# A graph-network kernel: splits put between ScalarE's normalising steps, half a batch norm on GpSimd, and the projection in two unrolled parts

## The reference, cut to what matters

```
h = relu(layernorm(x));  x = x + sage(relu-batchnorm of sage(h))      # two mean aggregations
h = relu(layernorm(x));  x = x + two hops of a relational layer (h)
h = relu(layernorm(x));  x = x + batchnorm(relu((h + A h) @ W1 + b1) @ W2 + b2)
h = relu(layernorm(x));  x = x + attention(h):
    w = softmax(h @ attn_w.T + attn_b);  xp = h + w @ node_anchor
    b = softmax(leaky(concat(h[src], h[dst]) @ edge_w.T + edge_b));  ep = b @ edge_anchor
    xp + 0.5 * (sum of ep at src + sum of ep at dst)
```

## Time and profile before

| | |
|---|---|
| median of 3 runs | 5902.55 us (5898.19 to 5908.68) |
| the profiled execution | 5876.22 us |
| its span in the profile | 5874.40 us |
| busy: PE, PEld, DVE, ACT, POOL | 59%, 40%, 40%, 23%, 38% |
| chain that ended last: PE, issue, POOL, DVE, ACT | 21%, 18%, 16%, 5%, 2% |

### The profile page before, as it was taken

One profiled execution on the slowest core, in us unless ns is written; L12 is line 12 of the kernel. 1 busy time (PEld: TensorE's weight loads), 2 busy tenths in 40 slices (PEclk: granted clock), 3 DMA queues, 4 the chain that ended last, 5 costly groups with the idle time before them and its releaser, 6 DMA issues.

```text
span 5874.4 us, 68831 instructions
## 1 busy us (share of the span) xinstructions
PE 3488.4 (59%) x18857; PEld 2341.4 (40%) x18858; DVE 2356.2 (40%) x6119; ACT 1354.9 (23%) x2986; POOL 2236.6 (38%) x2337
## 2 busy tenths in 40 slices
PE   5599997998633333333333333337994566655566
PEld 3255553444332222222333233333443455544455
DVE  7756566113322222222122222223116555555556
ACT  2555451001200000000000000001002555555555
POOL 3000000000366666665666666660001444444442
PEclk8699998998756666666555555558995777777777
DMA  2111113222522222222111111113220221212122
GB/s 70 52 68 46 67 45 129 94 87 87 160 56 67 69 67 67 70 66 68 46 45 46 46 46 46 46 45 115 108 87 17 44 45 43 45 41 41 43 50 53
DMA packets 264711, 371.64 MB, mean 63 GB/s; under 512 B 63252, under 2 KB 200251, under 8 KB 256299
## 3 DMA queue, kind: packets, MB, share of 16 engines
q1 hardware_dynamic: 186790, 251.51, 12.9%
q0 software_dynamic: 74464, 114.31, 8.7%
q10 hardware_dynamic: 3364, 4.69, 0.3%
HBM read 261.10 MB, written 109.21 MB: 63 GB/s over the span
## 4 chain that ended last, share of the span: by engine, by line
PE 21%; issue 18%; POOL 16%; another core or an unknown queue 9%; DVE 5%; DMA 2%; DVEq 2%; ACT 2%; ACTq 0%; POOLq 0%; SPq 0%
POOL GS L716 16%; PE psum L1296 7%; PE psum L1437 5%; PE psum L1242 3%; DMA GS<-xw_table,stage 2%; PE psum L1464 2%; DVEq L1779 1%; DVE GS L1779 1%; PE psum L1389 1%; PE psum L1390 1%; PE psum L1431 1%; PE psum L1221 1%; DVEq L1786 0%; ACT O L1056 0%
## 5 line engine op out<-in xcount | busy, mean ns | idle before, releaser
L716 POOL DMA_INDIRECT GS<-xw_table,stage x1664 | 1576.7, 948 | 2277.3 <-issue 1925.9
L1296 PE MATMUL psum<-HA,HT 128*128 128x512 fp8e4 (+1 forms) x5733 | 1253.7, 369 | 63.8 <-DVE HT L1962 63.8
L1242 PE MATMUL psum<-GS 128*128 128x96 f32 x3328 | 691.1, 382 | 712.7 <-DMA GS<-xw_table,stage 611.1
L716 POOL DMA_INDIRECT HA<-p_table,stage x624 | 603.3, 967 | 1213.6 <-DMA p_table<-HT 536.6
L1242 PEld LDWEIGHTS psum<-GS 128*128 128x128 f32 x3328 | 634.5, 287 | 765.7 <-issue 762.2
L1296 PEld LDWEIGHTS psum<-HA,HT 128*128 128x128 bf16 x5733 | 554.5, 100 | 642.8 <-DVE HT L1962 64.8
L1779 DVE TENSOR_SCALAR GS<-iota,HT,wt 128x96 f32<-128x96 f32 x1680 | 473.7, 349 | 449.8 <-issue 448.2
L1793 DVE TENSOR_TENSOR HA<-HA,psum 128x96 f32 x208 | 52.8, 254 | 1358.7 <-remote 859.4
L1221 PE MATMUL psum<-Wcat,HT 128*128 128x512 f32 x196 | 177.6, 1060 | 476.7 <-DVE HT L2255 443.4
L991 ACT ACTIVATE HA<-psum 128x392 fp8e4<-128x392 f32 x784 | 349.5, 494 | 345.5 <-PE psum L1201 332.3
L1201 PE MATMUL psum<-edge_cols 128*128 128x196 bf16 x1568 | 341.0, 351 | 39.1 <-ACT HA L991 23.6
(11 more groups left out here) (363 smaller groups left out, 4179.0 us busy)
## 6 DMA issues: line engine op xcount, KB each, us to landing
HT<-dst_rows SPq DMA_DIRECT2D x212, 256.0 KB
xw_table<-HT SPq DMA_DIRECT2D x100, 512.0 KB, 3.2
HA<-adj SPq DMA_DIRECT2D x26, 1600.0 KB, 6.3
adj<-HA SPq DMA_DIRECT2D x13, 3136.0 KB, 9.5
HA<-adj SPq DMA_DIRECT2D x26, 1536.0 KB, 9.7
GS<-xw_table,stage POOLq DMA_INDIRECT x1664
HA<-p_table,stage POOLq DMA_INDIRECT x624
h_table<-HA SPq DMA_DIRECT2D x4, 960.0 KB, 5.7
```

What stands on the lines that cost most here:

```text
L716: nc.gpsimd.indirect_dma_start(out=to, out_offset=None, in_=table, in_offset=bass.IndirectOffsetOnAxis(ap=idx, axis=0)).then_inc(done, 16)
L1242: last = nc.tensor.matmul(bank[h][:, 0:WINDOW], G3[g][:, j, :], S_pair[h][:, t, :], start=(t == 0), stop=(t == 2 * GT - 1))
L1296: last = nc.tensor.matmul(bank[s][:, 0:w], Hs4[:, b, t, :], adj_tile[s][:, b * GW:b * GW + w], start=(b == 0 and t == 0), stop=(b == SRCS ...
```

## The change

First group, splits and batch norms. `normalise_and_split` replaces `normalise` and `split` in the first and third layer: ACT normalises five blocks, splits ten, and so on, each split waiting only for the blocks that it reads. DVE no longer waits for all of `H` ahead of its part. `split(TO_SAGE2, ...)` starts when the first 25 blocks are there. POOL applies the first batch norm to blocks 25 to 49 and the second to blocks 32 to 49, while DVE does the others; the result goes straight into `H`. `O` is cleared by DVE, behind the split.

Second group, the projection. The last norm goes in two parts, blocks 0 to 27 (12 of them normalised by DVE) and 28 to 49 (12 by DVE), written out without loops. The projection takes four blocks at a time, in 13 steps, reads `H` without staging, and ACT copies the products too. `X = X + H` is one DVE step of 50 blocks.

```diff
+        blocks_in = lambda i: {PROJ: 4}.get(i, 1)
+        NORM_PARTS = ((slice(0, 28), slice(0, 12)), (slice(28, NB), slice(28, 40)))
+        BY_POOL = slice(32, NB)
...
@@ POOL
             gather_rest(REST_SAGE1, (h_table, P))
+            pool.wait_ge(bn_scaled, 1)
+            nc.gpsimd.tensor_tensor(H3[:, late_half, :], O3[:, late_half, :], in_late_half(sd[:, :]), ALU.mult).then_inc(bn_scaled, 1)
+            pool.wait_ge(bn_scaled, 2)
+            nc.gpsimd.tensor_tensor(H3[:, late_half, :], H3[:, late_half, :], in_late_half(mu[:, :]), ALU.add).then_inc(h_ready, 1)
...
-            pool.wait_ge(combined, 2 * HOP_BLOCKS)
-            nc.gpsimd.memset(O[:, :], 0.0).then_inc(rest_cleared, 1)
             gather_rest(REST_GIN, (h_table, P))
+            pool.wait_ge(bn_scaled, 3)
+            nc.gpsimd.tensor_tensor(T3[:, BY_POOL, :], T3[:, BY_POOL, :], in_blocks(sd[:, :]), ALU.mult).then_inc(bn_scaled, 1)
+            pool.wait_ge(bn_scaled, 4)
+            nc.gpsimd.tensor_tensor(X3[:, BY_POOL, :], X3[:, BY_POOL, :], T3[:, BY_POOL, :], ALU.add).then_inc(bn_scaled, 1)
@@ ACT, the projection
+            def copy_turned(m):
+                act.wait_ge(transposed, proj_before + m + 3)
+                act.wait_ge(multiplied, proj_before + m + 1)
+                nc.scalar.activation(tT[m % 2][:, 0:w], bank[6 + m % 2][:, 0:w], ACT.Copy).then_inc(t_copied, 1)
+            def copy_projected(m):
+                act.wait_ge(multiplied, proj_before + m + 3)
+                nc.scalar.activation(T[:, 4096 + m * 60:4096 + m * 60 + w], bank[2 + m % 2][:, 0:w], ACT.Copy).then_inc(evac_d, 1)
+            root_of(0)
+            normalise_four(3)
+            normalise_four(4)
+            copy_turned(0)
+            normalise_four(5)
+            copy_turned(1)
+            act.wait_ge(bn_scaled, 5)
+            copy_projected(0)
+            normalise_four(6)
+            for m in range(2, 6):
+                copy_turned(m)
+                copy_projected(m - 1)
+            root_of(1)
+            for m in range(6, 9):
+                normalise_four(m + 4)
+                copy_turned(m)
+                copy_projected(m - 1)
...
@@ PE, the projection
+            turn_normed(0)
+            for m in range(1, steps_of(PROJ)):
+                turn_normed(m)
+                project(m - 1)
+            project(steps_of(PROJ) - 1)
@@ DVE
-            wait_for_normed(1)
             split_h(TO_SAGE1)
...
-            for at, ready in zip(halves, (h_first, h_ready)):
-                ch(V.tensor_tensor(T3[:, at, :], O3[:, at, :], over_half(sd[:, :]), ALU.mult))
-                V.tensor_tensor(H3[:, at, :], T3[:, at, :], over_half(mu[:, :]), ALU.add).then_inc(ready, 1)
-            dve.wait_ge(h_ready, 2)
+            ch(V.tensor_tensor(H3[:, halves[0], :], O3[:, halves[0], :], over_half(sd[:, :]), ALU.mult))
+            V.tensor_tensor(H3[:, halves[0], :], H3[:, halves[0], :], over_half(mu[:, :]), ALU.add).then_inc(h_first, 1)
             split_h(TO_SAGE2)
...
-            wait_for_normed(4)
             split_h(TO_GIN)
-            dve.wait_ge(rest_cleared, 1)
+            dve.wait_ge(combined, 2 * HOP_BLOCKS)
+            ch(V.memset(O[:, :], 0.0))
...
-            for at in halves:
-                ch(V.tensor_tensor(T3[:, at, :], T3[:, at, :], over_half(sd[:, :]), ALU.mult))
-            ch(V.tensor_tensor(X3, X3, T3, ALU.add))
-            layer_norm()
+            dve.sem_inc(bn_scaled, 1)
+            mine = slice(0, BY_POOL.start)
+            ch(V.tensor_tensor(T3[:, mine, :], T3[:, mine, :], sd[:, :].unsqueeze(1).broadcast_to([P, mine.stop, P]), ALU.mult))
+            ch(V.tensor_tensor(X3[:, mine, :], X3[:, mine, :], T3[:, mine, :], ALU.add))
+            V.tensor_copy(iota49, iota[:, 0:49])
+            normalise_part(*NORM_PARTS[0])
+            dve.wait_ge(bn_scaled, 5)
+            normalise_part(*NORM_PARTS[1])
...
+            dve.wait_ge(h_ready, 6)
+            dve.wait_ge(h_act, 4 * NORM_ACT_STEPS + 3)
+            V.tensor_tensor(X3, X3, H3, ALU.add)
-            block_loop(PROJ, project_out, lambda b, s: V.tensor_copy(in_st[s][:, 0:2 * P], H[:, bass.ds(b * 2 * P, 2 * P)]))
+            dve.wait_ge(evac_d, steps_before(PROJ) + steps_of(PROJ) + 2)
```

More of the change, by code:

```diff
@@ L382, in gnn_stack @@
         hop_added = sem("hop_added")
-        rest_cleared = sem("rest_cleared")
+        bn_scaled = sem("bn_scaled")
         dst_in = [sem(f"dst_in{i}") for i in range(2)]
@@ L883, in stage_h @@
                 return nc.scalar.activation(in_st[s][:, 0:P], H[:, bass.ds(b * P, P)], ACT.Copy)
[L886 to L898, removed]
+            ten = lambda c: slice(c * 10, min(SRCS, c * 10 + 10))
@@ new lines, in high, with middle, normalise_and_split, five @@
+            def high(c):
+                nc.scalar.activation(Hs4[:, ten(c), 0, :], H3[:, ten(c), :], ACT.Copy).then_inc(split_high, 1)
+            def middle(q, c):
+                act.wait_ge(split_rest, 5 * q + c + 1)
+                nc.scalar.activation(Hs4[:, ten(c), 1, :], halves_of[c % 2][:, 0:ten(c).stop - ten(c).start, :], ACT.Copy).then_inc(split_mid, 1)
+            def normalise_and_split(q, norm, first, ready):
+                def five(i):
+                    for b in range(NORM_DVE + 5 * i, NORM_DVE + 5 * i + 5):
+                        last = nc.scalar.activation(H[:, b * P:(b + 1) * P], X[:, b * P:(b + 1) * P], ACT.Relu,
+                                                    bias=neg_mean[:, b:b + 1], scale=stat2[:, b:b + 1])
+                    last.then_inc(h_act, 1)
+                act.wait_ge(scales_ready, norm)
+                five(0)
+                act.wait_ge(h_first, first)
+                high(0)
+                act.wait_ge(h_ready, ready)
+                high(1)
+                middle(q, 0)
+                high(2)
+                middle(q, 1)
+                five(1)
+                act.wait_ge(h_act, NORM_ACT_STEPS * (norm - 1) + 2)
+                high(3)
+                middle(q, 2)
+                five(2)
+                five(3)
+                act.wait_ge(h_act, NORM_ACT_STEPS * norm)
+                high(4)
+                middle(q, 3)
+                middle(q, 4)
@@ L900, in turn_own, with split @@
+            def split(q, first, ready):
+                act.wait_ge(h_first, first)
+                high(0)
+                high(1)
+                middle(q, 0)
+                act.wait_ge(h_ready, ready)
+                for c in range(2, 5):
+                    high(c)
+                    middle(q, c - 1)
+                middle(q, 4)
             def turn_own(q, roots):
@@ L1034, in _ @@
             sqrt(stat2[:, :], stat[:, :], 2 * DENSE + 4)
[L1035 to L1039, removed]
+            normalise_and_split(TO_GIN, 3, 4, 4)
             relu_hidden()
@@ L1073, in _, with root_of, normalise_four @@
                 rows_ahead(0, 0, g)
-            sqrt(stat2[:, :], stat[:, :], 2 * DENSE + 6)
-            normalise(4)
+            proj_before = steps_before(PROJ)
+            def root_of(part):
+                at = NORM_PARTS[part][0]
+                sqrt(stat2[:, at], stat[:, at], 2 * DENSE + 6 + part)
+                act.wait_ge(scales_ready, 4 + part)
+            def normalise_four(m):
+                for b in projected(m):
+                    last = nc.scalar.activation(H[:, b * P:(b + 1) * P], X[:, b * P:(b + 1) * P], ACT.Relu,
+                                                bias=neg_mean[:, b:b + 1], scale=stat2[:, b:b + 1])
+                last.then_inc(h_act, 1)
+            def copy_turned(m):
+                w = len(projected(m)) * P
+                act.wait_ge(transposed, proj_before + m + 3)
+                act.wait_ge(multiplied, proj_before + m + 1)
+                nc.scalar.activation(tT[m % 2][:, 0:w], bank[6 + m % 2][:, 0:w], ACT.Copy).then_inc(t_copied, 1)
+            def copy_projected(m):
+                w = len(projected(m)) * 15
+                act.wait_ge(multiplied, proj_before + m + 3)
[17 more added lines that the diff above has]
+                copy_projected(m - 1)
+            for m in range(9, steps_of(PROJ)):
+                copy_turned(m)
+                copy_projected(m - 1)
+            copy_projected(steps_of(PROJ) - 1)
             act.wait_ge(zeros_done, 1)
```

72 lines of the change are left out of this document (50 added, 22 removed).

## The result

| | us |
|---|---|
| before, median of 20 runs | 5911.69 (5887.11 to 5918.23) |
| changed kernel, median of 20 runs | 5890.89 (5874.97 to 5904.19) |
| ratio | 0.9972, 95% interval 0.9963 to 0.9980 |
| profiled execution of the changed kernel | 5891.48 (span 5889.7) |

The ratio on record is not the quotient of the two medians, which would be 0.9965 (-20.8 us); the text goes by the recorded ratio, since it has the interval. Of 5902.55 us it is -16.5 us, with an interval of -21.8 to -11.8: faster. The forecast of 5881 (-21.6) lies at the interval's edge, and the cases of 5863.5, 5897 and 5958 lie outside.

The account below looks back on a forecast made before the run. Chains of waits, stage by stage, were taken as the bound, no engine being busy over 59%. Terms -0.6 - 8.6 + 5.3 - 17.7 = -21.6 us took the median from 5902.55 to 5881 us, range 5856 to 5892.

Parts of the forecast that it names:

- D: Second batch norm, last norm and projection: -17.7 us, with the projection starting earlier and TensorE the bound from there.
- A: Norm and split before the first layer: -0.6 us, only the earlier end of the split counting.
- B: First batch norm, shared by DVE and GpSimd: +5.3 us, since the two take turns.
- Rival 1: Both batch norms: DVE and GpSimd overlap, total -39.0 us, giving 5863.5 us; chance 0.30.
- C: Norm and split before the third layer: -8.6 us, from moving O's clearing to DVE (-3.2) and an earlier first split (-5.4).
- Taking turns from 4446.8: Second batch norm: DVE 4.4, GpSimd 4.9, DVE 4.4 us, ending at 4460.6, GpSimd's sum then beside one-input statistics.
- 50 blocks at 0.585: Projection: TensorE is the bound from its start, 0.585 us a block, 29.3 us in all.
- Rival 2: Projection becomes a ping-pong: 13 steps of 3.5 us are 46, giving 5897 us; chance 0.07.
- Rival 3: Attention loop falls back to 26.9 us an iteration, +77 us, giving 5958 us; chance 0.04.
- The sign that the prediction set for itself: Attention loop: prediction is wrong if the mean iteration moves by more than 0.2 us.

Follow-up runs that it names:

- s6: Changed kernel with the second batch norm on DVE alone, while GpSimd makes a one-input copy of 2304 elements; 5889.14 us, timed once.
- s8: Changed kernel with a two-element GpSimd memset before its scaling in the second batch norm, so DVE begins first; 5108.04 us, changed kernel 5106.91 to 5109.25.
- s4: Changed kernel with O cleared by GpSimd again before the third layer; 5844.82 us, timed once beside the kernel before at 5852.95.
- s9: s7 with TensorE's order in a projection step made two transposes, two products, two transposes, two products; 5084.37 us.
- s7: s5 with the first batch norm in five pieces of ten blocks, split steps between them; 5875.82 us, ratio 0.9940; again 5084.07 us, 0.9917.
- s1: Changed kernel with the first batch norm on DVE alone, in two halves; 5852.31 us, timed once beside the kernel before at 5852.95.
- s2: Changed kernel with the second batch norm on DVE alone, two steps of 50 blocks; 5830.04 us, timed once beside the kernel before at 5852.95.
- s5: Changed kernel with both batch norms on DVE alone, the second in pieces of 28, 10 and 12 blocks; 5869.83 us, ratio 0.9937; again 5092.51 us, 0.9931.
- s3: Changed kernel with GpSimd's part of the second batch norm waiting until DVE has scaled and added its 32 blocks; 5845.50 us, timed once.

## Why the prediction was right or wrong

**The step that failed is the order of the turns in D, and with it the pace of the projection.** The sign was right, and so was the mechanism that the engines exclude each other; the size was 3.2 us too large by the stages, 3.8 of it in D, with 0.6 back elsewhere. The forecast was -21.6, the stages give -18.4, the runs -16.5 (-21.8 to -11.8) in the first set, where the medians differ by 20.8, and -19.5 in the steadier one.

- **A**: -0.54 for -0.6. That the start of the split doesn't count held: TensorE's first matmuls come 5.6 us earlier after the norm's first step, and the one-hots only 0.54. The term itself was mis-sized (the split's end moves 1.17), and an idle time that was not in the sum took 0.62 of it back, so the agreement is partly luck.
- **B**: exclusion, turns and price were as forecast: 6.78 us for GpSimd's 3200 elements (6.8 taken), +4.9 for +5.3. The turns were over after 20.4 us (20.6), and TensorE followed 4.2 us behind them (4.5). That DVE came first here as assumed was no more asked for than in D. The price was a choice between bounds, and fell right by some luck. Rival 1 (the engines overlap, -39.0) falls here and in s6, s8.
- **C**: -8.85 for -8.6; s4 gives 3.2 of it to the memset, as forecast. That DVE's 5.4 us memset is hidden held too.
- **D** failed in two terms. First, "Taking turns from 4446.8: DVE 4.4, GpSimd 4.9, DVE 4.4": the order of the turns was assumed, from DVE to GpSimd, and not asked for. GpSimd began 0.02 us earlier, so both of its steps stood ahead of DVE's last: 18.5 us, not 13.7. s8 turns the order round: with DVE first the statistics begin 13.76 us after the scaling, as forecast, and the stage is 4.9 us shorter. Statistics paid 1.8 us back (5.50 for 28 where 7.3 had been taken from a loop with its turns: written out, one costs 0.196), so the start came at 29.35 instead of 26.7. Second, "50 blocks at 0.585": that pace was read off steps of two, and held for steps of four without a look at what the order does; it was 0.613, and the stretch 32.0 us for 30.8. s9 gives the step's pace back (0.587), though only 0.5 us of the stretch.
- **Rival 2** (ping-pong, 46 us) did not come: 32.0. **Rival 3** (attention loop at 26.9 us an iteration) neither: (1356.9 - 1352.4)/52 = 0.09 us an iteration, and 936.1 and 936.3 us for two kernels with different starts in the steadier set. The sign that the prediction set for itself, 0.2 us an iteration, was too fine for a single pair of profiles: with the loop unedited, s4 and s7 differ by (1360.8 - 1329.1)/52 = 0.61 us.

The forecast weighed B against the kernel before alone, and so did not say what GpSimd's part costs beside the same edit without it: 6.3 us in B (s1) and 4.7 in D (s2). Without it the second batch norm can also be cut in pieces, 29.35 - 18.68 = 10.7 us in D (s5). The change brought 19.5 us where the same kernel with DVE alone brings 35.0.

## What to carry to other kernels

Before work is given to GpSimd, look at what DVE does at that moment: if its step has two inputs and GpSimd's reads, the engines take turns and GpSimd's share is added to the chain at GpSimd's pace. Beside DVE's statistics GpSimd's sum cost nothing (s3). Not every one-input step is free, though: the TENSOR_SCALAR of the earlier trace rows and s4 waited out a memset, 3.40 us for 0.18. Where two engines must take turns, make the order certain, with a semaphore or by starting one earlier, since 0.02 us decided over 4.9. And judge a small change by its stages, between the same instructions: in the steadier set they agree with the medians to 1.1 us, while single profiled executions differed by 34 us in code that was not edited. The stages say what an edit does where it stands; whether the whole gains as much still needs several runs, as s8 shows.

## What the runs showed of the hardware that was not expected

**The kernel before took 5911 us in one set of runs and 5127 in another.** For the changed kernel, straight-line stages agree to a few hundredths: B 24.64 and 24.63, C 14.60 and 14.60, D 29.33 + 32.02 and 29.34 + 32.02 us. The loops do not: second layer with hop passes 3028.7 and 2670.9, attention loop 1356.9 and 936.1. Grouped rows of the hop passes' gathers on GpSimd (busy, mean ns, idle before and what ended it), the changed kernel in either set, from a window of 2000 us each:

```profile
L719 POOL DMA_INDIRECT GS<-xw_table,stage x1349 | 1276.8, 946 | 724.1 <-issue 418.1 <-remote 233.3 <-PE psum L1321 72.7
```

```profile
L719 POOL DMA_INDIRECT GS<-xw_table,stage x1585 | 1497.2, 945 | 503.8 <-issue 427.0 <-PE psum L1321 76.8
```

GpSimd runs nothing but these gathers there, and they take most of its time. One takes the same time (946 and 945 ns); the idle time before one is 724.1/1349 = 0.54 us in the slower set and 503.8/1585 = 0.32 in the quicker. Most of the difference, 233.3/1349 = 0.17 us, is idle time that the profile puts down to "remote", a name that it gives without saying more, and that is absent in the quicker set. DVE's TENSOR_SCALAR steps in the same windows (L1877, 349 and 354 ns) have 0.25 and 0.09 us of idle time each before them. The gathers are no slower, they come later. Why was not tried, and stays open. The chip alone need not be it: the record has the same chip number, 3, for the set of s1 to s4, with the kernel before at 5852.95, and for the one with 5127.51; whether that number names the same chip both times is not on record.

**GpSimd's lengths.** Two inputs, 2304 elements: 5.04 us alone (s3); one input: 2.10 us (s6). Per element that is 2.19 ns for the sum and 0.91 for the copy, and its memset, which reads nothing, has 0.85: the price comes with the second input. The Trainium skill, "GPSIMD Engine Reference", section Elementwise, has 4497 ns for 2048 elements of a sum; the estimate for 2304 from it is 5.06 us, and the trace agrees (5.04).
